# New shares of the quantisation levels, the first quarter of the convolution kernel ahead, and two orders at the end of a four-layer fused block

## What is computed

```
# layer 0: a state space kernel K (32 heads, 64 modes, length 512), a causal convolution over the
# features of each token, masked by a length; then an fp8 linear layer
K = 2*einsum('hn,hnl->hl', Cs, exp(P)).real
y = (conv(u_m, K) + u_m*D) * mask ;  x = x + y @ (w_fp8*scale).T
# layer 1: every sequence through the matrix of its adapter (16 of them, ids 1..14), then a gated
# FFN (hidden 1376) whose three matrices are first rounded to the 16 values of NF4 by blocks of 64
dq = NF4_CODE[searchsorted(bounds, w/absmax)]*absmax      # 15 bounds
x = x + (silu(c @ dq1.T) * (c @ dq2.T)) @ dq3.T
# layer 2: linear layer with low-rank experts (top 2 of 8), then attention over 128 slots and a gate
# layer 3: a gate per sequence and feature column, then base product, low-rank part and mixing
c = x*sigmoid(conv5(masked mean))[:, :, None]
H = c @ W + b ; z = c @ A
x = x + H + (z * p_mix) @ Bmat * scaling
```

## Time and profile before

| | |
|---|---|
| runs, us | 873.6, 868.88, 865.85; median 868.88 |
| the profiled execution | 865.41 us, its span 863.6 us |
| PE busy | 825.8 us (96%), 3325 records |
| DVE busy | 638.9 us (74%) |
| ACT busy | 415.8 us (48%) |
| POOL busy | 152.7 us (18%) |
| PE's granted clock | 9 or more tenths in all 40 slices |
| chain that ended last | PE 83%, DVE 8%, POOL and its queue 5% |

### The profile page before, as it was taken

How to read it: one execution, slowest core, us unless ns; L and a number is a source line. 1 busy time by engine, 2 the same in 40 slices (tenths; PEclk the granted TensorE clock), 3 DMA queues, 4 the chain that set the end, 5 groups by cost and what they waited for, 6 DMA issues and landing times.

```text
span 863.6 us, 10782 instructions
## 1 busy us (share of the span) xinstructions
PE 825.8 (96%) x3325; PEld 459.6 (53%) x3326; DVE 638.9 (74%) x981; ACT 415.8 (48%) x550; POOL 152.7 (18%) x162
## 2 busy tenths in 40 slices
PE   2499899999999999999999999999999999999998
PEld 2498799984444444444344444444455554543443
DVE  7899799969999999998999986343362462458445
ACT  5055188869787787886788730000011232245100
POOL 4100099101122211121122200002402022020000
PEclk9999999999999999999999999999999999999999
DMA  6696157920000001101010030013020000002022
GB/s 208 222 375 226 56 214 229 325 106 24 24 3 23 25 18 35 34 0 35 1 33 0 1 97 1 0 58 138 0 68 1 1 0 1 1 1 50 0 98 98
DMA packets 35151, 61.06 MB, mean 71 GB/s; under 512 B 6170, under 2 KB 8988, under 8 KB 34460
## 3 DMA queue, kind: packets, MB, share of 16 engines
q1 hardware_dynamic: 34232, 60.32, 20.6%
q0 software_dynamic: 352, 0.04, 0.2%
q10 hardware_dynamic: 516, 0.07, 0.0%
HBM read 50.90 MB, written 8.47 MB: 69 GB/s over the span
## 4 chain that ended last, share of the span: by engine, by line
PE 83%; DVE 8%; POOLq 3%; issue 2%; POOL 2%; ACT 1%; DMA 1%; SPq 0%; ACTq 0%; DVEq 0%
PE ps L969 81%; DVE acc L1608 3%; POOLq L685 2%; POOL Yp L687 1%; PE ps L1029 1%; PE ps L1301 1%; DVE W2T L1474 1%; DVE T L1608 1%; DVE W2T L1468 1%; DMA T<-kpad 0%; DVE W2T L1471 0%; DMA W2T<-in_log_dt 0%; DVE raw L1586 0%; DVE amax L1579 0%; POOLq L687 0%
## 5 line engine op out<-in xcount | busy, mean ns | idle before, releaser
L761 ACT ACTIVATE above<-raw,cst 128x1024 uint8<-128x1024 f32 (+2 forms) x225 | 267.8, 1233 | 48.6 <-DVE T L1608 20.0
L1608 DVE SCALAR_TENSOR_TENSOR acc<-above,acc 128x1024 f32<-128x1024 uint8 (+2 forms) x112 | 159.6, 1425 | 14.7 <-ACT above L761 11.4
L969 PE MATMUL ps<-Up,W2T 128*128 128x512 f32 (+1 forms) x404 | 160.6, 593 | 0.0
L969 PE MATMUL ps<-Up,W1T 128*128 128x512 f32 x344 | 155.5, 594 | 2.6 <-DVE Up L1707 2.2
L1608 DVE SCALAR_TENSOR_TENSOR T<-above,T 128x1024 f32<-128x1024 uint8 (+1 forms) x84 | 129.4, 1540 | 3.4 <-ACT above L761 0.5
L969 PEld LDWEIGHTS ps<-Up,W2T 128*128 128x128 f32 (+1 forms) x404 | 66.5, 177 | 86.4 <-issue 86.4
L969 PEld LDWEIGHTS ps<-Up,W1T 128*128 128x128 f32 x344 | 64.1, 190 | 81.6 <-issue 76.3
L969 PE MATMUL ps<-Yp,W3T 128*128 (+3 forms) x618 | 104.5, 322 | 1.6 <-POOL Yp L683 1.2
L969 PEld LDWEIGHTS ps<-Yp,W3T 128*128 128x128 f32 (+1 forms) x618 | 79.2, 192 | 23.1 <-issue 22.5
L969 PE MATMUL ps<-X,W3T 128*128 128x512 f32 (+2 forms) x184 | 78.7, 579 | 0.0
L969 PE MATMUL ps<-X,W2T 128*128 128x512 f32 x140 | 61.3, 594 | 0.0
(11 more groups left out here) (344 smaller groups left out, 977.1 us busy)
## 6 DMA issues: line engine op xcount, KB each, us to landing
W3T<-in_wa SPq DMA_DIRECT2D x8, 1024.0 KB, 7.2
raw<-in_w SPq DMA_DIRECT2D x20, 256.0 KB, 3.0
W3T<-kpad SPq DMA_DIRECT2D x9, 512.0 KB, 8.5
Up<-in_xconv SPq DMA_DIRECT2D x4, 1024.0 KB, 8.7
X<-in_xT SPq DMA_DIRECT2D x4, 1024.0 KB, 9.7
W1T<-in_wa SPq DMA_DIRECT2D x4, 1024.0 KB, 7.6
xkeep<-X SPq DMA_DIRECT2D x4, 1024.0 KB, 10.6
X<-xkeep SPq DMA_DIRECT2D x4, 1024.0 KB, 9.4
```

The source lines that it names most:

```text
L761: nc.scalar.activation(above[0:h, m % NAB, 0:w], raw[0:h, u % 2, 0:w], ACT.Relu, scale=STEEP, bias=cst[0:h, C_BND + i:C_BND + i + 1]).then ...
L969: return nc.tensor.matmul(o, l, r, start=start, stop=stop, **kw)
L1608: V.scalar_tensor_tensor(out=ac, in0=src, scalar=float(STEPS[i]), in1=ac, op0=ALU.min, op1=ALU.add).then_inc(s["m_used"], 1)
```

## The change

- `trig`, `pc` and the products are made for heads 0 to 7 first and then for heads 8 to 31. DVE writes the first quarter as `k0` (16 partitions, from PSUM bank 4) after two operations of the second part; SP writes it to `kpad` at once and issues strips 0 and 1. Before strip 2 it waits for `d_k` 2 and writes the other three quarters.
- The two `p_ord` products (`ranking`) run on PE behind the wait for strip 1, ahead of group 1. PE waits for `d_k` 1 at group 4.
- Levels: NF0 10 instead of 7; NAD 57 instead of 53, where the last four adapters have 4, 4, 5 and 3 and the others share 41.
- At the end base 4 is cut: its first product, the turn of the weights, its other three; then `ranks`, then base 5.
- The last block (outputs 12 to 15): before output 8 DVE multiplies X's four chunks by G into `xg` and the last block of `zq` by G (five products, `d_zp` 5). PE waits for that at base 12 and takes `xg` as operand; the outputs have one DVE operation each instead of two.

```diff
-        NCV, NF0, NAD, LATE = 8, 7, 53, 3
+        NCV, NF0, NAD, LATE = 8, 10, 57, 3
+        AD_END = [4, 4, 5, 3]
...
-            for q in range(4):
-                sp.dma_start(kr[:, q * HQ:(q + 1) * HQ, :], ksb[q * 32:q * 32 + LA, :, :]).then_inc(s[f"l_kp{q}"], 16)
+            sp.dma_start(kr[:, 0:HQ, :], k0).then_inc(s["l_kp0"], 16)
             sp.wait_ge(s["l_kpz"], 16)
             for g in range(HG):
...
+                if g == 2:
+                    sp.wait_ge(s["d_k"], 2)
+                    for q in range(1, 4):
+                        sp.dma_start(kr[:, q * HQ:(q + 1) * HQ, :], ksb[q * 32:q * 32 + LA, :, :]).then_inc(s[f"l_kp{q}"], 16)
...
+                if g == 1:
+                    ranking()
+                if g == 4:
+                    pe.wait_ge(s["d_k"], 1)
...
+                if n == GATED:
+                    pe.wait_ge(s["d_zp"], TB + 1)
...
-            for n in range(2, 5):
-                base(n)
+            base(2)
+            base(3)
+            base(4, range(0, 1))
             pe.wait_ge(s["d_w3"], 1)
...
-            base(5)
+            base(4, range(1, DC))
             for half in range(2):
                 ranks(half)
+            base(5)
...
+            for part in (slice(0, HQ), slice(HQ, S)):
+                n = part.stop - part.start
+                wide = [P, n, LA]
+                V.tensor_tensor(trig[:, part, 0:LC], trig[:, part, 0:LC], dec[:, part, 0:LC], ALU.mult).then_inc(s["g_dec"], 1)
+                tt(pc[:, part], trig[:, part, CMULT:], al[:, part].unsqueeze(2).to_broadcast(wide), ALU.mult)
+                if part.start:
+                    dve.wait_ge(s["p_k"], 1)
+                    V.tensor_tensor(k0, ps[0:LA, 4, 0:HQ * LC].rearrange("p (h c) -> p h c", c=LC), kdk[0:LA], ALU.add
+                                    ).then_inc(s["d_k"], 1)
+                tt(pq[:, part], trig[:, part, LC:CMULT], be[:, part].unsqueeze(2).to_broadcast(wide), ALU.mult)
+                tt(pc[:, part], pc[:, part], pq[:, part], ALU.add)
+                V.tensor_tensor(pc[:, part], pc[:, part], dec[:, part, LC:], ALU.mult).then_inc(s["d_pp"], 1)
...
+                if n == 2 * DC:
+                    last = tok(TB - 1)
+                    for c in range(DC):
+                        tt(xg[:, c, :], X[:, c, last], G[:, last], ALU.mult)
+                    V.tensor_tensor(zq[:, last], zq[:, last], G[:, last], ALU.mult).then_inc(s["d_zp"], 1)
...
-                tt(tmp[n % 2], ps[:, BANKS3[n % 8], :], G[:, tok(tb)], ALU.mult)
-                V.scalar_tensor_tensor(out=results[n], in0=tmp[n % 2], scalar=b3[:, oc:oc + 1],
+                ungated = ps[:, BANKS3[n % 8], :]
+                if n < GATED:
+                    tt(tmp[n % 2], ungated, G[:, tok(tb)], ALU.mult)
+                V.scalar_tensor_tensor(out=results[n], in0=tmp[n % 2] if n < GATED else ungated, scalar=bias,
                                        in1=X[:, oc, tok(tb)], op0=ALU.add, op1=ALU.add).then_inc(s["d_o"], 1)
```

More of the change, by code:

```diff
@@ L162, in build @@
         n0 += 2 * HQ * LC
+        k0 = w2f[0:LA, 5120:5120 + HQ * LC].rearrange("p (h m) -> p h m", h=HQ)
         sm = w2f[:, n0:n0 + 32 * S].rearrange("p (k h) -> p k h", h=S)
@@ L345, in build @@
         zq = yf[:, 0:TOK]
+        xg = uf[:, 0:DC * TW].rearrange("p (c n) -> p c n", c=DC)
+        GATED = (TB - 1) * DC
         results = [region[:, i * TW:(i + 1) * TW] for region, k in
@@ L390, in build @@
         AD_LAST = K_FFN0[-1] + NAD
-        K_AD = [K_FFN0[-1] + (a + 1) * NAD // ADAPT for a in range(ADAPT)]
+        AD_EVEN = NAD - sum(AD_END)
+        K_AD = [K_FFN0[-1] + ((a + 1) * AD_EVEN // (ADAPT - 4) if a < ADAPT - 4 else AD_EVEN + sum(AD_END[:a + 5 - ADAPT]))
+                for a in range(ADAPT)]
         W12 = LEV * NH
@@ L990, in _ @@
             pe.wait_ge(s["g_dec"], S + 1)
+            for h in range(HQ):
+                last = mm(ps[0:LA, 4, h * LC:(h + 1) * LC], pc[:, h, :], trig[:, h, 0:LC], True, True)
+            last.then_inc(s["p_k"], 1)
+            pe.wait_ge(s["d_pp"], 2)
+            pe.wait_ge(s["g_dec"], S + 2)
             pe.wait_ge(s["d_kz"], 1)
             for i in range(HQ):
-                for q in range(4):
+                for q in range(1, 4):
                     h = q * HQ + i
@@ L996, in _, with ranking @@
             last.then_inc(s["p_k"], 1)
[L997 to L1001, removed]
+            def ranking():
+                pe.wait_ge(s["d_ones"], 1)
+                pe.wait_ge(s["d_oneh"], 1)
+                mm(ps[0:1, 5, 0:NB], cst[0:NB, C_PCOL:C_PCOL + 1], oneh[:, 0:NB], True, True)
+                mm(ps[0:1, 5, NB:NB + ADAPT + 1], ones[0:NB, 0:1], oneh[:, NB:], True, True).then_inc(s["p_ord"], 1)
             def turn_unit(u):
@@ L1023, in turn_unit @@
                     elif n + m < 2:
-                        pe.wait_ge(s["d_k"], 1)
+                        pe.wait_ge(s["d_k"], 2)
                         pe.wait_ge(s["a_kk"], 1)
@@ L1358, in aux_rank, with entering, base @@
                 last.then_inc(s["p_rk"], 1)
-            def base(n):
+            def entering(n, c, cols):
+                return xg[:, c, cols.start - (TB - 1) * TW:cols.stop - (TB - 1) * TW] if n >= GATED else X[:, c, cols]
+            def base(n, some=range(DC)):
                 tb, oc = n // DC, n % DC
+                if n == GATED:
+                    pe.wait_ge(s["d_zp"], TB + 1)
                 if n < 2:
@@ L1373, in base @@
                     return
-                for c in range(DC):
-                    mm(ps[:, BANKS3[n % 8], :], l3w[:, c, oc * P:(oc + 1) * P], X[:, c, tok(tb)], c == 0, False)
+                for c in some:
+                    mm(ps[:, BANKS3[n % 8], :], l3w[:, c, oc * P:(oc + 1) * P], entering(n, c, tok(tb)), c == 0, False)
             def spread_gates(pair):
@@ L1404, in lift @@
                         for c in range(DC):
-                            mm(ps[:, b, part], l3w[:, c, oc * P:(oc + 1) * P], X[:, c, cols], c == 0, False)
+                            mm(ps[:, b, part], l3w[:, c, oc * P:(oc + 1) * P], entering(n, c, cols), c == 0, False)
                         mm(ps[:, b, part], bm4[g, :], zq[g, cols], False, True).then_inc(s["p_oh"], 1)
@@ L1546, in _ @@
             dve.wait_ge(s["g_dec"], S)
[L1547 to L1553, removed]
-            dve.wait_ge(s["g_dsk"], 3)
+            dve.wait_ge(s["g_dsk"], 3)
+            for part in (slice(0, HQ), slice(HQ, S)):
[10 more added lines that the diff above has]
+                V.tensor_tensor(pc[:, part], pc[:, part], dec[:, part, LC:], ALU.mult).then_inc(s["d_pp"], 1)
+            dve.wait_ge(s["p_k"], 2)
             V.tensor_tensor(ksb, ps[:, 6, 0:HQ * LC].rearrange("p (h c) -> p h c", c=LC), kdk, ALU.add).then_inc(s["d_k"], 1)
@@ L2029, in _ @@
                 tb, oc = n // DC, n % DC
+                bias = b3[:, oc:oc + 1]
+                if n == 2 * DC:
[3 more added lines that the diff above has]
+                    V.tensor_tensor(zq[:, last], zq[:, last], G[:, last], ALU.mult).then_inc(s["d_zp"], 1)
                 if n == TB * DC - 1:
@@ L2033, in _ @@
                         dve.wait_ge(s["p_oh"], i + 1)
-                        tt(tmp[n % 2][:, part], ps[:, LAST_BANKS[i], part], G[:, cols], ALU.mult)
-                        V.scalar_tensor_tensor(out=results[n][:, part], in0=tmp[n % 2][:, part], scalar=b3[:, oc:oc + 1],
+                        V.scalar_tensor_tensor(out=results[n][:, part], in0=ps[:, LAST_BANKS[i], part], scalar=bias,
                                                in1=X[:, oc, cols], op0=ALU.add, op1=ALU.add).then_inc(s["d_o"], 1)
```

## The result

| | before | after |
|---|---|---|
| runs, median | 867.11 us (865.43 to 873.6, 20 runs) | 870.62 us (866.86 to 875.06, 20 runs) |
| ratio, 95% interval | | 1.0037 (1.0025 to 1.0049) |
| profiled execution, its span | 865.41, 863.6 | 871.63, 869.8 |
| mean granted clock of it | 1.00 | 0.994 |

The account below looks back on a forecast made before the run. PE was taken to bound the kernel, with gains only in its gaps and at its two ends. Terms +0.86, -1.24, -0.3, -0.94, -0.46 gave -2.1 us, forecast median 866.8 us; range 862 to 871.5, forecast's own 865 to 868.5.

Parts of the forecast that it names:

- The start, the transfers: Start and convolution: strip 0 lets PE start 2.47 us earlier, later `d_w0` delays strip 5; whole start +0.86 us.
- The short wait at group 11: Convolution: PE reaches group 11 before strip 11 has landed and waits until 63.79 us.
- The rival that strips are no limit: Convolution: PE is not held by strips, the start gives -2.1 us, total 863.9 us; chance 0.2.
- The start, the pace behind the wait: Convolution, behind the new wait at group 5: the sum added nothing beyond the wait's length.
- a rival (+1.57, chance 0.1): Convolution: the wait at group 5 slows PE's next two groups, +1.57 us, total 868.4 us; chance 0.1.
- First FFN to adapters, -1.24: Gap between first FFN and adapters: fewer DVE operations before the last `X` bring it 1.24 us earlier.
- The bound 0: Gap between first FFN and adapters: no gain if the extra levels make DVE late for the last X.
- Adapters to `up`, 0: Adapter stage to first `up`: ACT's last copy 0 to 0.6 us late against PE, taken as 0.
- The -0.3 of the first silu: First silu: ACT has two levels fewer there, so PE's 0.3 us wait goes.
- The end, -0.94 and -0.46: End: base 5 covers PE's wait before the last lift, -0.94 us; last output without product with G, -0.46 us.

Follow-up runs that it names:

- the start alone: The kernel before with only the start changed (first quarter ahead, four-quarter order of the writes, `ranking` moved): 870.23 us, ratio 1.0033.
- SP's new order: The kernel before with the changed start, strips 5 and 6 issued ahead of `d_w0`, weights and X, X's other blocks one group later: 864.81 us, ratio 0.997.
- the levels ahead: The kernel before with only the new level shares, the first FFN's ten levels put in its first 12 steps: 867.97 us, ratio 1.0003.
- the shares alone: The kernel before with only the new shares of the levels (NF0 10, NAD 57, last adapters 4, 4, 5, 3): 869.44 us, ratio 1.003.

## Why the prediction was wrong, by its own steps

- **The start, the transfers: right with the start alone, 1.4 us too small in after.** PE's start at 32.29 (forecast 32.35), `d_w0` at 40.73 (40.5), strip 5 issued 42.16 (41.93), the wait at group 5 at 2.18 us with the start alone (2.5). In the profiled execution of after the landing took 8.5 us instead of 6.9 and the wait 3.9; why it landed later is not shown. The short wait at group 11 did not come, since PE was later there. The rival that strips are no limit fell for this order of transfers; with SP's new order the start gave 2.15 us, the 2.1 that this rival had.
- **The start, the pace behind the wait: the step that failed.** The sum put the cost of the new wait beyond its length at nothing. It was +1.72 us with the start alone and +2.94 in after, where PE ran behind the wait at a granted clock of 0.50. I had it as a rival (+1.57, chance 0.1) and argued against it that PE waited 2.2 us at `hidden` without such a step. That was one trace. Seven of 13 show the step there. With the fall the start cost 2.31 us alone and 5.06 in after. No term let a second fall (adapters, +1.63) in. The measured 870.6 us lies inside my wide range (862 to 871.5), which is luck: the case that I had for this cause ends at 868.4, and the forecast's own range (865 to 868.5) missed.
- The Trainium skill (TensorE: Matmul & The Clock Gate, The HAM clock gate) says that an idle stretch sets PE back to half its clock. I set it aside because the clock column of before read 1.00 throughout, though its first two groups took 6.55 us and began at the pace of half a clock. The traces agree with it in the two levels, 1.00 and 0.50, and not as a rule for a single wait: the same 2.15 us gave either, and a fall came behind a wait of 0.94 us at the first lift in one trace, while 3.09 us ahead of the adapters in another went without.
- **First FFN to adapters, -1.24: wrong, +0.25 to +0.35.** I said the three added levels fit because DVE was busy for 19.48 of 26 us. That is a mean; what counts is the last four steps. DVE's timeline of after there:

```profile
102.29 1.23 DVE L1649 TENSOR_TENSOR acc<-acc,amax 128x1024 f32<-128x1024 f32 x1
103.55 0.75 DVE L1720 SCALAR_TENSOR_TENSOR X<-ps,wsc,X 128x512 f32<-128x512 f32 x1
105.93 0.70 DVE L1640 TENSOR_SCALAR W2T<-above 128x1024 f32<-128x1024 uint8 x1 [1.62 <-issue]
106.66 1.41 DVE L1720 SCALAR_TENSOR_TENSOR X<-ps,wsc,X 128x512 f32<-128x512 f32 x2
107.99 1.22 DVE L1643 SCALAR_TENSOR_TENSOR W2T<-above,W2T 128x1024 f32<-128x1024 uint8 x1
109.24 0.75 DVE L1720 SCALAR_TENSOR_TENSOR X<-ps,wsc,X 128x512 f32<-128x512 f32 x1
109.90 1.22 DVE L1643 SCALAR_TENSOR_TENSOR W2T<-above,W2T 128x1024 f32<-128x1024 uint8 x1
```

  At output 12 stand three register loads of the order of the sequences, which count as no busy time (1.62 us of "issue"). They and the levels between the outputs keep DVE behind PE; the last `X` ends at 111.90, 2.50 us behind PE's last product at 109.40, where before it was 2.16. The bound 0 that I gave was the right end, and the reason beside it ("the extra levels make DVE late") was the true case. With the levels ahead the gap shrank by 1.4 us against before.
- **Adapters to `up`, 0: wrong by size.** With the shares alone the first `up` waits 1.33 us for ACT; I had counted 0 to 0.6 and taken 0. The term too small was the three copies behind ACT's last level, 3.06 us instead of 1.5. In after it waits 0.28, since PE itself is late there; most of the stage's +2.63 is the clock (1.63) and a PE wait of 0.96 that the profile gives only as "issue", whose cause I did not find. The -0.3 of the first silu came.
- **The end, -0.94 and -0.46: right in sum, -1.53 for -1.40.** PE's last product ends 0.81 us earlier relative to the turn, and behind it the span is 0.72 us shorter (2.88 instead of 3.60). One DVE operation is left there, without the product with G:

```profile
866.96 0.48 DVE L2075 SCALAR_TENSOR_TENSOR above<-ps,b,X 128x256 f32<-128x256 f32 x1 [2.06 <-PE ps L978]
```

Without the two half-clock stretches of after the difference of the profiled spans would be +1.6 us (6.2 less 2.94 and 1.63), and the forecast was 2.1 below zero. So the other terms were wrong by 3.7 together: 1.6 in the gap ahead of the adapters, 1.0 in the adapters, and 1.3 in the start, where strip 5 landed later than counted; the end gave back 0.1.

## What to carry to other kernels

Put what a later stage needs early in the queue ahead of what it doesn't need yet: moving two strips ahead of X turned the start from +2.3 us into -2.2. Before adding work to an engine with idle time, count the last steps ahead of the point where others wait for it, and spend its spare time once only. Price a new wait of PE at its length plus a possible stretch at half clock, and look at several traces before saying that a wait of this length costs nothing.

## What the hardware showed that I had not expected

- A PE wait of 1 to 4 us may or may not cost the clock. Falls followed waits of 0.94, 1.2, 2.15, 2.18, 3.1, 3.2, 3.8 and 3.9 us; each cost 1.3 to 3.0 us, more than the wait itself in two places (1.70 behind 0.94, 2.95 behind 1.42 and 1.22). Much of the scatter of the kernel's runs goes with it: 866.0 us where the mean clock is full, 868.3 where it is 0.998. A loss of 1.7 us in 865 makes a mean clock of 0.998.
- Products without use in a wait kept the clock there: 8 records (3.65 us) in place of a wait of 3.9 us, and the next stage started 2.56 us earlier.
- The clock column may not be a full witness: in the window of 36 to 38 us of before 9 records ran, the pace of a clock of 0.50, and the column reads 1.00. The cause is not shown.
- 16 KB writes to `kpad` issued behind two strips took 3.5 to 3.7 us to land (issued 29.9 to 30.6), against 1.5 to 1.6 with nothing ahead of them.
- Ahead of output 12, where DVE makes three register loads, it stands idle for 1.4 to 1.6 us by the profile, put down to "issue" in after and to PE in the two DVE timelines with the levels ahead. The chain that ended last has about 1.0 us of it in pieces of the loads' own line (L1715 of after).
